# Hybrid attention and feed-forward kernel: empty instructions that place TensorE's instruction stream in blocks of 256

## What is computed

```python
def step(carry, qkv):                       # for each token t, each batch and head
    S_K, C_QV, G = carry
    k_C = einsum('bhk,bhkv->bhv', k_t, C_QV)
    G = G + k_t[..., :, None] * k_C[..., None, :]
    S_K = S_K + k_t[..., :, None] * k_t[..., None, :]
    C_QV = C_QV + q_t[..., :, None] * v_t[..., None, :]
    S_C = einsum('bhkj,bhjv->bhkv', S_K, C_QV)
    o_t = einsum('bhk,bhkv->bhv', q_t, S_C - G)
```

## Time and profile before

| | us |
|---|---|
| median of 3 runs | 1000.53 |
| lowest, highest | 1000.41, 1001.06 |
| the profiled execution's own time | 1001.22 |
| its span, first to last instruction | 999.5 |
| PE busy in it | 976.4 |
| DVE (VectorE) busy | 615.7 |
| ACT (ScalarE) busy | 487.2 |
| POOL (GpSimdE) busy | 112.8 |

### The profile page before, as it was taken

The page is one execution under the profiler, slowest core; times in us unless marked ns, Lnnn a source line. Parts: engine busy times, 40 slices in busy tenths (PEclk is TensorE's granted clock), DMA queues, the critical chain, the costliest instruction groups (busy, mean ns, idle before and its releaser), DMA issues.

```text
span 999.5 us, 41893 instructions
## 1 busy us (share of the span) xinstructions
PE 976.4 (98%) x18990; PEld 889.9 (89%) x18990; DVE 615.7 (62%) x1314; ACT 487.2 (49%) x941; POOL 112.8 (11%) x178
## 2 busy tenths in 40 slices
PE   8999899999999999999999999999999999999998
PEld 6888789999899999999998999899998998799997
DVE  6888877863446555455456644655545566667763
ACT  5676776643344433443353344343444335547663
POOL 2362322320000000000000000000000000112240
PEclk9999999999999999999999999999999999999999
DMA  9432112143323433343432442443343355322321
GB/s 324 137 83 85 64 64 85 65 148 107 121 75 118 148 122 108 129 130 108 130 109 93 155 140 72 133 142 108 109 130 129 108 159 164 114 90 74 127 75 53
DMA packets 76610, 115.84 MB, mean 116 GB/s; under 512 B 8848, under 2 KB 63504, under 8 KB 75408
## 3 DMA queue, kind: packets, MB, share of 16 engines
q1 hardware_dynamic: 76160, 113.15, 34.4%
q10 hardware_dynamic: 272, 0.00, 0.0%
HBM read 60.17 MB, written 52.95 MB: 113 GB/s over the span
## 4 chain that ended last, share of the span: by engine, by line
PE 93%; DVE 3%; issue 1%; ACT 1%; DMA 1%; POOL 0%; SPq 0%; POOLq 0%; DVEq 0%; ACTq 0%
PE bank L262 7%; PE bank L1269 6%; PE bank L264 6%; PE bank L263 6%; PE bank L1295 5%; PE bank L1280 4%; PE bank L1259 4%; PE bank L1329 4%; PE bank L1306 3%; PE bank L860 3%; PE bank L862 3%; PE bank L1377 3%; PE bank L1317 3%; PE bank L1378 3%; PE bank L1284 3%; PE bank L1260 3%
## 5 line engine op out<-in xcount | busy, mean ns | idle before, releaser
L1648 DVE STREAM_TRANSPOSE k<-kt 128x512 f32<-128x512 f32 x64 | 43.2, 694 | 101.2 <-ACT kt L1513 101.0
L1513 ACT COPY kt<-bank 128x512 f32<-128x512 f32 x64 | 37.6, 587 | 131.9 <-PE bank L264 131.9
L1676 DVE TENSOR_TENSOR ot_lo<-bank,ot_hi 128x512 fp32r<-128x512 f32 x64 | 41.2, 686 | 94.9 <-ACT ot_hi L1536 94.8
L1518 ACT COPY qt<-bank 128x512 f32<-128x512 f32 x64 | 37.5, 587 | 100.2 <-PE bank L264 100.2
L1523 ACT COPY v_all<-bank 128x512 f32<-128x512 f32 x64 | 37.5, 586 | 93.0 <-PE bank L1261 93.0
L262 PE MATMUL bank<-ln_xhi,wq_hi 128*128 128x256 f32 x256 | 73.8, 288 | 1.0 <-issue 1.0
L1329 PE MATMUL bank<-wo_hi,ot_hi 128*128 128x256 f32 x256 | 74.8, 292 | 0.0
L1280 PE MATMUL bank<-qt,state_s 64*64 64x64 f32 x2048 | 73.0, 221 | 1.5 <-issue 1.1
L1284 PE MATMUL bank<-qt,state_z 64*64 64x64 f32 x2048 | 73.1, 221 | 0.5 <-issue 0.5
L262 PE MATMUL bank<-ln_xhi,wk_hi 128*128 128x256 f32 x256 | 73.5, 287 | 0.0
L1280 PEld LDWEIGHTS bank<-qt,state_s 64*64 64x64 f32 x2048 | 66.2, 134 | 8.1 <-issue 2.3
(11 more groups left out here) (171 smaller groups left out, 2864.3 us busy)
## 6 DMA issues: line engine op xcount, KB each, us to landing
k_rows_scratch<-k SPq DMA_DIRECT2D x32, 512.0 KB, 3.4
k<-k_rows_scratch SPq DMA_DIRECT2D x128, 128.0 KB, 2.9
landed<-u_rows_scratch SPq DMA_DIRECT2D x124, 128.0 KB, 2.9
u_rows_scratch<-C_turned_u SPq DMA_DIRECT2D x30, 512.0 KB, 3.4
ln_xn<-x_rows_scratch SPq DMA_DIRECT2D x88, 128.0 KB, 3.0
x_rows_scratch<-B_turned SPq DMA_DIRECT2D x8, 512.0 KB, 2.6
x_rows_scratch<-C_turned SPq DMA_DIRECT2D x8, 512.0 KB, 4.0
xres<-in_L_attn_a_x_dram SPq DMA_DIRECT2D x7, 512.0 KB, 9.7
```

## The change

In ten turns a directive stands ahead of the first product of one part of the projection: ahead of x = 3 in turn 0, and ahead of x = 2 (the second half) in turns 3, 6, 9 and so on to 27. It asks the loader to put in as many empty instructions (no-operations) as bring the next instruction to a given place modulo 256 of PE's final stream; the default is that PE's sequencer then walks through all of them, up to 255. Nothing else of the program is changed.

```diff
--- before.py
+++ after.py
@@ -1002,6 +1002,10 @@
             turned_again = sc_a.rearrange("p m h t -> p (m h t)").rearrange("p (t m d) -> p t m d", t=4, m=PAIRS)
             turned_u = place("C_turned_u", 96, [P, 4, PAIRS, 32])
             OWN_TILE = CHUNKS - 2
+
+            FETCH = 256
+            TO_HALF, FROM_LAST = 307, 436
+            PLACE = {0: 190 - FROM_LAST, 3: 140 + TO_HALF, **{j: 132 + TO_HALF for j in range(6, CHUNKS - 4, 3)}}
 
 
             w1t_again = place("D_w1t", 24, [P, DC, FF], FP32R)
@@ -1431,6 +1435,8 @@
                             pe.wait_ge(a_masked, 2 * j + x + 1)
                         elif blk:
                             pe.wait_ge(q_done if even else k_done, 4 * blk + x - 1)
+                        if j in PLACE and x == (2 if j else 3):
+                            pe.addr_align(FETCH, PLACE[j] % FETCH)
                         if not blk:
                             up(x if even else 4 + x)
                         elif even:
```

## The result

The changed kernel takes 1080.88 us (median of 3 runs, 1080.65 to 1084.43) against 1000.53. The ratio is 1.081, with a 95% interval of 1.079 to 1.083. It is slower by 80 us; 1082 was forecast.

The account below looks back on a forecast made before the run. PE's own stream bounds the kernel, with 9.5 us lost in gaps. The terms -9 + 83.4 - 6.5 + 14 = +81.9 on the profiled 1001.22 gave 1083.1, and 0.7 less for the median 1082 us; range 990 to 1130.

Parts of the forecast that it names:

- fewer gaps: PE's issue gaps at 256-instruction block boundaries, 9.5 us up to turn 28, nearly all go by placement: -9 us.
- 1042 empty instructions: Padding at the ten directives, walked through by PE's sequencer at 80 ns each: +83.4 us, ends 53.1 and 114.6.
- cover: Sequencer's lead over PE at each directive hides 0.65 us of the walk, not 2.1: ten times, -6.5 us.
- clock: PE's granted clock may fall in each stop, slowing the 24 products behind: +14 us, between nothing and 29.
- The price: Time of one empty instruction on PE's sequencer: 80 ns, the middle of 51 and 110 from semaphore instructions.
- the step behind it: Gaps in PE's stream fall on instruction 194 or 195 modulo 256, so a block boundary lies there.
- The rule of the Trainium skill: Crossing a 16 KiB block boundary is mostly hidden; by it the -9 term would be 0, the sum 9 us higher.
- The bottom rival: Empty instructions on PE as cheap as matmuls, 7.3 ns, 1.1 us exposed in all: 992.6 us, chance 0.18.
- the floor of 17 to 21 ns: Rival: an empty instruction on PE costs what ACT's and DVE's semaphore instructions last: 1002.7 to 1006.9 us, chance 0.09.
- The prediction's estimate of 17 ns: Sequencer's issue floor of about 20 cycles at 1.2 GHz as price of an empty instruction: would make 1002.4 us.

Follow-up runs that it names:

- the jumping kernel: The change with max_nops=0, so the sequencer jumps over the empty instructions at the same ten places instead of walking through them: 991.52 us, ratio 0.989 to before.
- the pair that differs by 64 in place: Two kernels that jump over the padding: one with the change's places, 991.52 us, the other with all places moved on by 64, 1006.9 us.
- the run moved on by 64: The jumping kernel with all places moved on by 64: 1006.9 us, ratio 1.007 to the kernel before.
- the one added in turn 30: Jump of a further directive, in a run that also moved turn 0's place in the jumping kernel: 992.49 us, ratio 0.992 to before.

## Why the prediction was right

The time, 1080.9, is 1.1 us from the forecast of 1082, but this is better than its terms, which were off by several us each and in opposite directions. By the profiled executions, whose spans differ by 79.7 us:

| term | forecast | measured | from |
|---|---|---|---|
| fewer gaps | -9 | about -10 | span of the jumping kernel less that of before, 989.4 - 999.5 |
| 1042 empty instructions | +83.4 | +77 | 0.074 us each |
| cover | -6.5 | about -8.5 | 77 less the 68.6 of stops |
| clock | +14 | about +21 | PE busy 993.8 against 972.8 without stops |
| sum | +81.9 | 79.5 | |

Two of these, -10 and +21, lean on the jumping kernel's run. The price is measured by itself; the cover is only what is left of it beside the stops.

*Fewer gaps.* Right, and so was the step behind it: that the gaps stand at instruction 194 or 195 modulo 256 and that turns which start at places 131 to 237 are free. (The prediction counts 194 and 195 in the program's own stream; the places count in the final one, in which each instruction's number is 62 higher, so that the boundary is at place 0. Turn 3 starts at 69 in the one and at 131 in the other.) The turns of the change say so (19.94, 19.93, 19.87), and the pair that differs by 64 in place says it by itself. With it the cause is shown, as far as place decides it. The trace of before bears out that PE waits there for its block: between 247 and 830 us its fourteen longest gaps all stand at that number, and each ends 2.2 to 2.8 us after a packet of the instruction queue starts (the one of 484.43 after that of the earlier trace rows). That the packet comes late because it is asked for only on entry into the block before it wasn't tested.

*The rule of the Trainium skill* that a crossing is mostly hidden (Runtime: NRT & Kernel Launch, "Instruction fetch mechanics") doesn't hold for this kernel: 10 us come and go with the place of the crossings.

*The price.* The step that rested on the least was the choice of 80 ns between ends of 51 and 110, from the semaphore instruction as the nearest row. It came to 74. The bottom rival, as cheap as a matmul at 7.3 ns, is out by ten times, and the floor of 17 to 21 ns by about four: on PE an empty instruction takes as long as about ten matmuls or weight loads. The prediction's estimate of 17 ns from figures of the Trainium skill (Runtime: NRT & Kernel Launch, "Instruction fetch mechanics", about 20 cycles; Advanced Engine Details and Errata, "Clock Domains", 1.2 GHz) is out by four times as well. Why an empty instruction takes 74 ns no run shows, so that 80 came so near is in part luck.

*The cover.* The mechanism was right (the moved wait leaves 0.65 us of a lead of 2); the run with the directive ahead of the wait gave back 1.5 us a stop in nine of the ten, 1.4 expected. The size was low by 2 us in all. More than half of that is turn 0, where 155 empty instructions took 11.4 us but the stop only 9.5; its first empty instruction starts 1.8 us ahead of the stop, and with the directive ahead of the wait the stop was no shorter, so its wait had let the sequencer go sooner. The other nine had about 0.7 us each. The rule "0.65 us, ten times" was read off one turn.

*The clock.* This was the worst sized term. I put the middle of nothing and 24 products at half the clock. In the trace 18 of the 24 ran at the lower level, 0.21 us in place of 0.12, which is 1.6 us in turn 9. PE's busy time grew by 21 us over ten stops. About 3 us of that are turn 0, where the low clock lasted 13.6 us and reached past the products into `u_and_s` (64 passes in 3.46 us, 1.75 in later turns); the other nine, where it lasted 6.8 us with PE at work in 3.2 to 4.2 of them, make up the rest, some 2 us each. The middle was too low by 7 us, which the price's 6 us happened to balance.

## What to carry to other kernels

Where an engine stops for "issue" amid equal instructions, look whether the stops stand at one number modulo 256 in its stream; if they do, placing the blocks is worth trying, and a bad place makes the kernel slower than no placing at all (1006.9 us here). Placing must not be paid for on the path: here an empty instruction on TensorE's sequencer cost 0.074 us, about ten of the 64x64 passes' 7.3 ns, and a jump over all of them 0.17 us. Before hiding anything behind a queue's lead, ask where the sequencer itself last had to wait, since the lead counts from there.

## What the runs showed of the hardware

- An empty instruction on PE takes 0.074 us from start to start, though its record lasts 13 ns.
- A jump over 97 to 110 slots within a block took 0.17 to 0.18 us; the one added in turn 30 took 0.32. The one whose padding reached across a boundary took 2.5 us, and 2.7 in the run moved on by 64.
- The granted clock fell to 0.50 about 3.2 to 3.7 us into nine stops of 6.4 to 7.4 us and stayed there for 6.8 us, about half of it with PE at work; in the stop of 9.5 us it fell after 1.9 us and stayed low for 13.6. With stops of 1.8 us it fell four times in eight, 0.8 to 1.3 us after their end, for about 3.4 us. Before the change an idle end of 4.0 us had shown no fall.
